# Cross-attention, two layers on one core: score matmuls by pairs of heads with the query's parts stacked on 128 rows, and x's low parts moved from VectorE to GpSimd

## The reference, cut to what matters

```python
q = hidden_state @ Wq + bq
k = encoder_hidden_state @ Wk + bk
v = encoder_hidden_state @ Wv + bv
scores = einsum('bkgld,bksd->bkgls', q, k) * scale + mask
attn = softmax(scores)
out = einsum('bkgls,bksd->bkgld', attn, v)
x = layernorm(out @ Wo + bo + hidden_state) * gamma + beta
```

## Time and profile before

| | |
|---|---|
| median of 3 runs | 1743.74 us (1743.04 to 1747.58) |
| the profiled execution's own time | 1745.89 us |
| its span, first to last instruction | 1744.1 us |
| PE, DVE, POOL, ACT busy | 1712.8, 1165.5, 1066.8, 581.5 us |
| granted clock of TensorE, mean | 0.995 of full speed |

### The profile page before, as it was taken

How to read it: one execution, slowest core, us unless ns; L and a number is a source line. 1 busy time by engine, 2 the same in 40 slices (tenths; PEclk the granted TensorE clock), 3 DMA queues, 4 the chain that set the end, 5 groups by cost and what they waited for, 6 DMA issues and landing times.

```text
span 1744.1 us, 22384 instructions
## 1 busy us (share of the span) xinstructions
PE 1712.8 (98%) x8449; PEld 1429.8 (82%) x8449; DVE 1165.5 (67%) x1106; ACT 581.5 (33%) x669; POOL 1066.8 (61%) x592
## 2 busy tenths in 40 slices
PE   6999999999999999999999999999999999999998
PEld 6788888888888788888888877888888888888887
DVE  7899888888888666565656578446644664466443
ACT  4344454444444533333434223122312231223110
POOL 1677878777788966575756553445734573457331
PEclk9999999999999999999999999999999999999999
DMA  8342344323335677777776856556545654565332
GB/s 238 99 111 73 88 104 105 85 71 86 80 81 162 198 237 223 227 231 222 248 219 224 263 176 194 174 169 185 173 152 169 185 170 154 169 183 171 130 110 84
DMA packets 278127, 280.11 MB, mean 161 GB/s; under 512 B 62330, under 2 KB 230404, under 8 KB 278020
## 3 DMA queue, kind: packets, MB, share of 16 engines
q1 hardware_dynamic: 276672, 276.97, 52.3%
q10 hardware_dynamic: 1348, 1.71, 0.3%
HBM read 175.81 MB, written 102.76 MB: 160 GB/s over the span
## 4 chain that ended last, share of the span: by engine, by line
PE 72%; DVE 9%; POOL 8%; issue 4%; ACT 3%; DMA 2%; SPq 1%; POOLq 0%; DVEq 0%; ACTq 0%
PE ps L53 23%; PE ps L54 23%; PE ps L55 23%; POOL pT0l L1381 2%; POOL pr L1385 1%; PE ps L712 1%; PE ps L720 1%; POOL xb L1407 1%; DVE pT1r L1138 1%; DVE pr L1127 1%; DVE small L1107 1%; DVE pT0r L1138 1%; ACT pT1h L881 1%; DVE xT1r L1040 1%; DVE xT0r L1040 1%
## 5 line engine op out<-in xcount | busy, mean ns | idle before, releaser
L1458 POOL TENSOR_TENSOR x2Tl<-x2r,x2Th 128x1024 fp32r<-128x1024 f32 x31 | 74.6, 2405 | 274.2 <-ACT x2Th L973 274.2
L1235 DVE STREAM_TRANSPOSE x2r<-xd 128x1024 f32<-128x1024 f32 x32 | 68.9, 2154 | 200.1 <-PE ps L55 200.1
L1390 POOL TENSOR_TENSOR pr<-pr,small 128x1024 f32<-128x1024 f32 x64 | 122.0, 1906 | 98.6 <-DVE small L1133 98.5
L973 ACT CAST x2Th<-x2r 128x1024 fp32r<-128x1024 f32 x32 | 33.7, 1053 | 366.5 <-DVE x2r L1235 366.5
L1385 POOL TENSOR_TENSOR pr<-pr,small 128x1024 f32<-128x1024 f32 x64 | 122.0, 1906 | 8.7 <-DVE small L1111 6.2
L1407 POOL TENSOR_TENSOR xb<-xb,bo 128x1024 f32<-128x1024 f32 x32 | 77.9, 2436 | 69.2 <-DMA xb<-in_x_dram 69.2
L1107 DVE TENSOR_REDUCE small<-pr 128x16 f32<-128x1024 f32 x64 | 78.0, 1219 | 45.7 <-ACT pr L852 45.7
L1421 POOL TENSOR_TENSOR y<-y,bet 128x1024 f32<-128x1024 f32 x31 | 74.4, 2400 | 55.7 <-DVE y L1153 55.7
L53 PE MATMUL ps<-wo0h,oc0l 128*128 128x512 f32 x256 | 101.7, 397 | 1.7 <-DVE wo0l L1064 1.7
L1153 DVE TENSOR_TENSOR y<-y,gam 128x1024 f32<-128x1024 f32 x32 | 56.0, 1751 | 70.6 <-ACT y L894 70.6
L53 PE MATMUL ps<-wo0h,oc1l 128*128 128x512 f32 x256 | 101.6, 397 | 0.4 <-DVE y L1190 0.4
(11 more groups left out here) (379 smaller groups left out, 5446.3 us busy)
## 6 DMA issues: line engine op xcount, KB each, us to landing
xr<-in_x_dram SPq DMA_DIRECT2D x128, 128.0 KB, 2.9
o_scratch<-ot SPq DMA_DIRECT2D x256, 64.0 KB, 1.8
ocr<-o_scratch SPq DMA_DIRECT2D x16, 1024.0 KB, 7.9
xb<-in_x_dram SPq DMA_DIRECT2D x32, 512.0 KB, 6.2
a_scratch<-ost SPq DMA_DIRECT2D x64, 256.0 KB, 3.4
b_scratch<-ost SPq DMA_DIRECT2D x64, 256.0 KB, 5.6
xd<-x_scratch SPq DMA_DIRECT2D x128, 128.0 KB, 2.9
raw<-b_scratch SPq DMA_DIRECT2D x64, 256.0 KB, 5.9
```

The lines of the kernel that those rows point to most:

```text
L1235: nc.vector.transpose(x2r[:].rearrange("p k (t j) -> p t k j", t=TPB), xd[:].rearrange("p t (i k) -> p t k i", k=KT)).then_inc(x2_turned, 1)
L1390: nc.gpsimd.tensor_tensor(heads(v), heads(v), mx.unsqueeze(2).to_broadcast([P, TPB * GRP, KEYS]), ALU.subtract)\
L1458: nc.gpsimd.tensor_tensor(x2T[1][:], x2r[:], f32(x2T[0][:]), ALU.subtract).then_inc(x2_lo, 1)
```

## The change

The score matmuls of four heads become matmuls of two heads. `qs` of a unit is still two tiles, now called `a` and `b`: tile `a` holds the high part of the first two heads' query (64 rows) on its own rows, and their low part on the other 64 rows; tile `b` the same for the other two heads. `kb` has four parts: two with the high keys on all 128 rows, and two with the low keys on those 64 rows that hold the query's high part and zeros on the others. So one matmul on 128 rows adds high by high and low by high, and a second one high by low. For each group of tokens and each pair of heads these are 2 matmuls of 128 columns: 16 in a slot in place of 12 of 256.

For this ACT and DVE write each half of the query by itself, the key tiles `kst` and the scratch tensor hold the parts three times (four in `kst`), and the loads of keys take three parts in place of two.

x's low part in the attention is computed on POOL, as its first step in an odd slot. The Wq groups 6 and 7 are split in slots 3 and 5 (before: both in slot 1), and the last Wo group at the end of slot 63 (before: 64).

```diff
--- before.py
+++ after.py
@@ -96,12 +96,12 @@
         wkr, wvr = at("wk0r", 168, [P, KT, KV0]), at("wv0r", 152, [P, KT, KV0])
         wk = [at("wk0h", 176, [P, KT, KV0], F32R), at("wk0l", 168, [P, KT, KV0], F32R)]
         wv = [at("wv0h", 184, [P, KT, KV0], F32R), at("wv0l", 152, [P, KT, KV0], F32R)]
-        kst = [at(f"kst{h}", 136 + 2 * h, [P, BATCH, 2, KEYS], F32R) for h in range(2)]
+        kst = [at(f"kst{h}", 130 + 4 * h, [P, BATCH, 4, KEYS], F32R) for h in range(2)]
         vst = [at(f"vst{r}", 140 + 2 * r, [P, KVH0, 2, HD0], F32R) for r in range(2)]
         kf, vf = at("kf", 202, [P, 2, CTX]), at("vf", 204, [P, 2, KV0])
 
-        qs = [[at(f"qs{i}{x}", 152 + 4 * i + 2 * j, [P, TPB, P], F32R) for j, x in enumerate("hl")] for i in range(2)]
-        kb = [at(f"kb{i}", 160 + 2 * i, [P, GRP, 2, KEYS], F32R) for i in range(2)]
+        qs = [[at(f"qs{i}{x}", 152 + 4 * i + 2 * j, [P, TPB, P], F32R) for j, x in enumerate("ab")] for i in range(2)]
+        kb = [at(f"kb{i}", 160 + 2 * i, [P, 4, 2, KEYS], F32R) for i in range(2)]
         vb = [at(f"vb{i}", 164 + 2 * i, [P, 2, 2, P], F32R) for i in range(2)]
         pr = [at(f"pr{i}", 168 + 4 * i, [P, GRP, TPB, KEYS]) for i in range(2)]
         pTr = [at(f"pT{i}r", 176 + 8 * i, [P, 2, GRP, P]) for i in range(2)]
@@ -214,7 +214,7 @@
             return (2, 3) if u == 0 else ()
 
         def wq_late(u):
-            return (4, 5) if u == 0 else (6, 7) if u == 1 else ()
+            return (4, 5) if u == 0 else (6,) if u == 3 else (7,) if u == 5 else ()
 
         def half(i):
             return slice(KT // 2 * i, KT // 2 * (i + 1))
@@ -224,7 +224,7 @@
             return 4 * (t + 1) + g // 2 if g % 2 == 0 and t + 1 < NBLK else None
 
         def wo_groups(u):
-            return (u - (UNITS - 7),) if UNITS - 7 <= u <= UNITS else ()
+            return (u - (UNITS - 7),) if UNITS - 7 <= u < UNITS else ()
 
         def chunk0(u):
             i, r = divmod(u - 2 * KT - 14, 4)
@@ -285,27 +285,29 @@
                 sp.wait_ge(k_hi, h + 1)
                 sp.wait_ge(k_lo, h + 1)
                 for a in range(4):
-                    sp.dma_start(d["kv"][h, :, :, a, :P].rearrange("b p c -> p b c"),
+                    sp.dma_start(d["kv"][h, :, :, a, :2 * P].rearrange("b p c -> p b c"),
                                  f32(kst[h][32 * a:32 * (a + 1)]).rearrange("p b x s -> p b (x s)")).then_inc(kv_st, 16)
             def store_v():
                 for r in range(2):
                     sp.wait_ge(v_hi, r + 1)
                     sp.wait_ge(v_lo, r + 1)
                     for h in range(2):
-                        sp.dma_start(d["kv"][h, :, :, :, P + 64 * r:P + 64 * (r + 1)].rearrange("b p g c -> (b p) g c"),
+                        sp.dma_start(d["kv"][h, :, :, :, 2 * P + 64 * r:2 * P + 64 * (r + 1)].rearrange("b p g c -> (b p) g c"),
                                      f32(vst[r][:, 4 * h:4 * (h + 1)]).rearrange("p g x d -> p g (x d)")).then_inc(vv_st, 16)
 
             def load_k(u):
                 t, g = divmod(u, KT)
                 for j in range(GRP):
-                    sp.dma_start(f32(kb[u % 2][32 * j:32 * (j + 1), j]).rearrange("p x s -> p (x s)"),
-                                 d["kv"][g // 4, t // 2, :, g % 4, :P]).then_inc(k_ld[u % 2], 16)
+                    x = 1 - j // 2
+                    sp.dma_start(f32(kb[u % 2][32 * j:32 * (j + 1), x:x + 3, j % 2]),
+                                 d["kv"][g // 4, t // 2, :, g % 4, KEYS * x:KEYS * (x + 3)].rearrange("p (x s) -> p x s", x=3))\
+                        .then_inc(k_ld[u % 2], 16)
 
             def load_v(u):
                 t, g = divmod(u, KT)
                 for a in range(4):
                     sp.dma_start(f32(vb[u % 2][32 * a:32 * (a + 1), :, :, 32 * a:32 * (a + 1)]).rearrange("p c x d -> p (c x) d"),
-                                 d["kv"][g // 4, t // 2, :, g % 4, P:].rearrange("p (q d) -> p q d", d=HD0))\
+                                 d["kv"][g // 4, t // 2, :, g % 4, 2 * P:].rearrange("p (q d) -> p q d", d=HD0))\
                         .then_inc(v_ld[u % 2], 16)
 
             def load_norm():
...
@@ -641,17 +643,19 @@
                 if 1 <= u <= UNITS:
                     v = u - 1
                     if u < UNITS:
-                        pe.wait_ge(q_lo, v + 1)
+                        pe.wait_ge(q_lo, 2 * (v + 1))
                     pe.wait_ge(k_ld[v % 2], 16 * GRP * (v // 2 + 1))
                     after(pe, s_read, v - 1)
                     if v == 1:
                         pe.wait_ge(vfull, 2)
                     if u == UNITS:
                         half_tile(0, range(3))
-                        pe.wait_ge(q_lo, v + 1)
+                        pe.wait_ge(q_lo, 2 * (v + 1))
                     for m in range(TPB):
-                        last = three(nc, S[v % 2][:, 256 * m:256 * (m + 1)], [qs[v % 2][x][:, m] for x in (0, 1)],
-                                     [kb[v % 2][:, :, x] for x in (0, 1)], True, True)
+                        for h in range(2):
+                            for x in (3 - 3 * h, 1 + h):
+                                last = nc.tensor.matmul(S[v % 2][:, 256 * m + P * h:][:, :P], qs[v % 2][h][:, m],
+                                                        kb[v % 2][:, x].rearrange("p j s -> p (j s)"), start=x in (0, 3), stop=x in (1, 2))
                     last.then_inc(scores, 1)
                 if u < UNITS:
                     query(range(6, KT))
...
@@ -836,8 +840,10 @@
             split_wq(0)
             for h in range(2):
                 act.wait_ge(kfull, h + 1)
-                nc.scalar.copy(kst[h][:, :, 0, :].rearrange("p b (r i) -> p b r i", r=2),
-                               kf[:, h].rearrange("p (r b i) -> p b r i", r=2, b=BATCH)).then_inc(k_hi, 1)
+                for x in (1, 2):
+                    last = nc.scalar.copy(kst[h][:, :, x, :].rearrange("p b (r i) -> p b r i", r=2),
+                                          kf[:, h].rearrange("p (r b i) -> p b r i", r=2, b=BATCH))
+                last.then_inc(k_hi, 1)
             split_wq(1)
             for r in range(2):
                 act.wait_ge(vfull, r + 1)
@@ -866,15 +872,16 @@
                 if u < UNITS:
                     act.wait_ge(q_done, u + 1)
                     after(act, scores, u - 1)
-                    nc.scalar.activation(qs[u % 2][0][:], Q[u % 2].rearrange("p (n m) -> p m n", m=TPB), ACT.Identity,
-                                         bias=bq[:, u % KT:u % KT + 1]).then_inc(q_hi, 1)
+                    for h in range(2):
+                        own = slice(64 * h, 64 * (h + 1))
+                        nc.scalar.activation(qs[u % 2][h][own], Q[u % 2][own].rearrange("p (n m) -> p m n", m=TPB), ACT.Identity,
+                                             bias=bq[own, u % KT:u % KT + 1]).then_inc(q_hi, 1)
                     for g in wq_late(u):
                         split_wq(g)
+                    if u == UNITS - 1:
+                        split_wo(KT - 1)
                     if u - 2 * KT in (6, 7):
                         norm_rows(u - 2 * KT - 6)
-                if u == UNITS:
-                    for g in wo_groups(u):
-                        split_wo(g)
                 if 2 <= u < UNITS + 2:
                     v = u - 2
                     act.wait_ge(p_turned, v + 1)
@@ -1084,10 +1091,11 @@
             split_wq(0)
             for h in range(2):
                 dve.wait_ge(k_hi, h + 1)
-                nc.vector.tensor_tensor(kst[h][:, :, 1, :].rearrange("p b (r i) -> p b r i", r=2),
-                                        kf[:, h].rearrange("p (r b i) -> p b r i", r=2, b=BATCH),
-                                        f32(kst[h][:, :, 0, :]).rearrange("p b (r i) -> p b r i", r=2), ALU.subtract)\
-                    .then_inc(k_lo, 1)
+                for x in (0, 3):
+                    last = nc.vector.tensor_tensor(kst[h][:, :, x, :].rearrange("p b (r i) -> p b r i", r=2),
+                                                   kf[:, h].rearrange("p (r b i) -> p b r i", r=2, b=BATCH),
+                                                   f32(kst[h][:, :, 1, :]).rearrange("p b (r i) -> p b r i", r=2), ALU.subtract)
+                last.then_inc(k_lo, 1)
             dve.wait_ge(bv_ld, 16)
             for r in range(2):
                 dve.wait_ge(v_done, r + 1)
@@ -1099,8 +1107,6 @@
                                         f32(vst[r][:, :, 0, :]), ALU.subtract).then_inc(v_lo, 1)
 
             def slot(u):
-                if 1 <= u <= UNITS and (n := next_x(u - 1)) is not None:
-                    split_x(n)
                 if 2 <= u < UNITS + 2:
                     v = u - 2
                     dve.wait_ge(exped, v + 1)
@@ -1138,13 +1144,18 @@
                     nc.vector.transpose(pTr[v % 2][:].rearrange("p b j n -> p b (j n)").rearrange("p b (h i) -> p h b i", i=32),
```

(23 more changed lines are left out.)

4 lines of the change are left out of this document (2 added, 2 removed).

## The result

The changed kernel takes 1803.06 us (median of 5 runs, 1801.51 to 1805.89) against 1743.74 (5 runs, 1743.04 to 1747.58): ratio 1.0332, interval 1.0319 to 1.0345. The forecast was 1784, range 1764 to 1804. The profiled span went from 1744.1 to 1801.3, +57.2 where the sum said +40.4. So the sign and the main mechanism hold, and about 17 us of it are not in the sum.

A forecast was written before the change was run, and what follows sets the result against it. PE was taken as only just the bound, level with a ring through POOL, ACT and DVE. Start −2, ring +40.6, exit +0.9, last slots +2.6 and Wo's last group −1.7 make +40.4: 1784 us, range 1764 to 1804.

The forecast's parts named there:

- own range: Spread of the forecast case alone, from x's low part at 3.02 or 1.91, score bounds and start: 1768 to 1802 us.
- the ring: Attention loop: POOL max-subtract, ACT exp, DVE sum, mask, maximum, POOL again; a pair of slots 16.49 us, forecast 17.87.
- Score matmul 0.110: Attention scores on PE: 128-column matmuls start 0.110 us apart, like the fp32 transposes; +0.33 us per PE slot.
- x's low part 2.36 in a full odd slot, nothing gained on DVE: On POOL it adds 2.36 us by starts, DVE gives nothing back; odd slot 8.46 us instead of 7.08.
- Even slot untouched, 9.41: Attention slot where DVE also turns an x tile: six steps and their order unchanged, so it stays 9.41 us.
- Wq's groups in slots 3 and 5, +1: Two weight splits at the ends of these early attention slots add 1 us in all.
- The last 8 slots have no x, PE is the bound again: 8 × 0.33 = +2.6: End of the attention: each slot grows only by PE's dearer scores, +2.6 us, bounds −3.1 to +3.8.
- the exit +0.9: Leaving the x slots: PE's scores start later after POOL's max-subtract, and one odd slot more is longer than PE's; +0.9 us.
- 1: Rival: a 128-column score matmul costs what a 512-column one does, PE slot 10.48, 1882 us; chance 0.08.
- 2: Rival: x's subtraction finds room on POOL beside the attention loop, 1740 us with 0.065 per score matmul; chance 0.05.
- 3: Rival: PE's saving arrives, 0.065 us per score matmul, −25 over 64 slots, 1715 us; chance 0.05.
- Rival 4: PE's waits in each attention slot lower its clock; if it stayed at 0.50, more than +300 us; chance 0.03.

The follow-up runs named there:

- E5: Changed kernel with three of each four of x's low parts moved on POOL from the odd slot into its wait of the even slot; 1779.14 us.
- E2: Kernel before the change with only x's low part moved to POOL, first in the odd slot; scores, query parts and weight groups as before; 1782.80 us.
- E6: Changed kernel with a third, narrower matmul (64 moving or 64 weight columns) in each score sum, scores not right; one run, 1812.78 us.
- E1: Changed kernel with x's low part of the attention back on DVE, first in its slot; 1816.13 us.
- E3: Changed kernel with Wo's low parts in slots 57 to 64 on POOL behind pT's low part, in the slot of the high part; 1803.09 us.
- E7: Changed kernel with Wo's low parts on POOL behind pT's low part, one slot after their high part (slots 58 to 65); 1805.85 us.
- E9: Changed kernel with Wo's low part on DVE ahead of the query's two low parts in slots 57 to 64, not behind them; 1802.55 us.
- E11: Changed kernel with Wo's last group split in slot 64 again, as before the change, not in slot 63; 1800.50 us.

## Why the prediction was right, and where not

The time lies in the range, but near its end, and that it does is in part luck. 1803.06 is 1 us below the upper bound of 1804 and 1 above the "own range" of 1768 to 1802. That upper end was priced with x's low part at 3.02 us in all 28 slots; it took 2.38 to 2.40 in a full odd slot, and what filled the room was a loss in the last slots that no term had. (The terms of that range, all on one side, add up to 1762 and 1805, not to 1768 and 1802.) The mechanism holds by itself: +46.0 us of the +57.2 stand between slots 2 and 54, where +40.6 was forecast.

- *PE and the ring are level, the ring is late next:* right. E5 and E2 show both sides: with x's part out of the odd slots PE bounds at 8.65, with it the ring does at 17.8 to 18.0 a pair.
- *Score matmul 0.110:* measured 0.112 to 0.114, PE slot 8.65 for 8.59. That it goes by the columns of weights is shown by E6.
- *x's low part 2.36 in a full odd slot, nothing gained on DVE:* right, 8.44 for 8.46 (8.47 in E2). Beside the split query parts it is otherwise: E1 shows 13 us for x's part being off DVE. The chunk slots are 10.58 for 10.66, the coefficients cost 1.1 where 2.4 was forecast.
- *Even slot untouched, 9.41:* it is 9.54 on average, +3 us over 24 of them. "The query's parts: nothing on the ring" was nearly true; E2, without them and the new score block, has 9.31 to 9.37 in nearly all. I took each half at 0.63 by starts, they are 0.77.
- *Wq's groups in slots 3 and 5, +1:* the first four distances are 39.7 where 36.7 was forecast. The one in slot 5 took 3.12 us, again behind POOL's pT low part, and PE's stall of slot 3 was still 1.8 us with a granted clock of 0.50 after it. Another 1.5 us go in slot 44, after PE's wait for a chunk slot: the clock is 0.50 there for some 6 us, and E3, E7, E9 and E11, in which that slot is 8.43 to 8.46, did not lose them. The excess here (3.0 in the first slots, 3.1 in the even ones, 1.5 in slot 44), less what the coefficients, the odd and the chunk slots came in under (some 2), is the 5.4 us by which the 26 pairs exceed the forecast; the start adds 0.9 (−1.1 for −2).
- *"The last 8 slots have no x, PE is the bound again: 8 × 0.33 = +2.6", with the exit +0.9 and −1.7 for Wo's last group:* the step that failed. These terms made +1.8 and measured +12.3 (57.2 + 1.1 − 46.0), 10.5 of the 16.8 us that the sum lacks. The prediction has no term for Wo's subtraction on DVE in these slots: by calling PE the bound it takes it to cost what it cost before, 1.36, although the split query parts ahead of it move it by 0.9 us and POOL's pT low part began only 0.61 behind it. The runs showed 3.03 us for it and a ring of 9.70, above PE's 8.65; without it on DVE (E3, E7) or with it ahead (E9) the 9.70 are gone. The prediction had used that very meeting for x's subtraction and did not look for it a second time.
- *Rivals:* 1, 2 and 3 are out by PE's slot and by POOL's full odd slots. Rival 4 happened in small. Up to slot 54 PE waits six times for 1.3 to 1.8 us (59.5, 99.2, 327.4, 365.4, 403.3 and 441.2), and after each the granted clock is 0.50 (1.2 GHz) for some 3 to 6 us: 60 to 72 us has PEclk 0.72 (0.76 before), 440 to 456 has 0.79 (1.00 before). Apart from the first slots and slot 44 the ring hides it.
- *Busy times:* POOL's grew by 46.7 us, where 50 was forecast, DVE's by 40.2, where "about 7" was. The two query parts are +50.5 for 45, and Wo's subtractions, of which nothing was said, +9.5; the rest of that difference is not followed up here. DVE's busy time costs nothing by itself.

Windows of the changed kernel (us, busy of each engine with instructions, PEclk, DMA share, GB/s):

```profile
60.00:72.00 12.00, 12.00 (x50) 10.30 (x50) 9.78 (x11) 4.34 (x5) 10.09 (x6) 0.72 0.39 103
...
440.00:456.00 16.00, 14.78 (x67) 12.70 (x68) 11.99 (x13) 7.17 (x9) 12.80 (x7) 0.79 0.22 60
```

## What to carry to other kernels

Where engines pass one buffer round a ring, follow the ring slot by slot and ask of each moved operation in which slot it stands: with three of four of the same 2.4 us moved out of the full slot into one with a wait, the time fell by 24 us and that slot did not grow. When an operation ahead of another grows by some tenths, list every pair of operations on DVE and GpSimd that met in the trace and see whether their order turns; the one that comes second paid here, and it matters whether that one is in the ring. When every matmul has its own weights and at most 128 moving columns, as here, count loads of weights, not columns streamed.

## What the runs showed of the hardware

- Two-source DVE operations against GpSimd's: second to come, DVE's 1.36 became 3.03 (0.43 us behind), 3.02 and 1.99 (0.99 behind a max-subtract). Each time DVE ends 1.36 us after a point 0.28 to 0.29 us ahead of the recorded end of GpSimd's (596.24 + 3.03 − 1.36 = 597.91, against 595.81 + 2.38 = 598.19; in E9 601.69 against 601.98). In E1 it is 0.27 (270.60 + 3.02 − 1.36 = 272.26, against 272.53). Either GpSimd's record outlasts its hold by about 0.3 us, or the first 0.3 us of DVE's operation do not need what GpSimd holds; no run here tells the two apart.
- A matmul with 64 moving columns and full weights is no quicker than one with 128 (0.109, 0.112); one with 64 weight columns takes 0.058.
- In the changed kernel a stretch at a granted clock of 0.50 followed each of PE's six waits of 1.32 to 1.82 us up to slot 54, and none of those of 0.4 to 0.8. It does not follow every time: in E9 the waits of 1.32 and 1.50 us at 327.6 and 365.5 had one behind them, those of 1.33 and 1.65 at 403.4 and 441.5 had none.
